# Flamingo-style stack of four gated attention and feed-forward pairs: softmax sums inverted on token partitions

## The reference, cut to what matters

```
x = x + tanh(g_xattn[l]) * attention_l(layernorm(x), ctx, ctx, ...)
x = x + tanh(g_ffn[l])   * feed_forward_l(layernorm(x), ...)

# attention, layers 0, 1 and 3: 16 heads of 8 features
scores  = einsum('bhqd,bhkd->bhqk', Q, K) ...   # with bias, causal mask or none
weights = softmax(scores, axis=-1)
out     = einsum('bhqk,bhkd->bhqd', weights, V)  # then Wo
# layer 2: 4 query heads of 32 features, one key and value head
```

## Time and profile before

| what | value |
|---|---|
| median of 3 runs | 1038.44 us (1036.83 to 1040.66) |
| profiled execution, span from first to last instruction | 1044.5 us |
| profiled execution's own device time | not recorded apart from its span |
| TensorE matmul busy | 876.9 us (84%) |
| TensorE weight load busy | 566.3 us (54%) |
| VectorE busy | 790.5 us (76%) |
| ScalarE busy | 492.8 us (47%) |
| GpSimd busy | 302.3 us (29%) |

### The profile page before, as it was taken

One profiled execution on the slowest core, in us unless ns is written; L12 is line 12 of the kernel. 1 busy time (PEld: TensorE's weight loads), 2 busy tenths in 40 slices (PEclk: granted clock), 3 DMA queues, 4 the chain that ended last, 5 costly groups with the idle time before them and its releaser, 6 DMA issues.

```text
span 1044.5 us, 19277 instructions
## 1 busy us (share of the span) xinstructions
PE 876.9 (84%) x7316; PEld 566.3 (54%) x7316; DVE 790.5 (76%) x1849; ACT 492.8 (47%) x753; POOL 302.3 (29%) x324
## 2 busy tenths in 40 slices
PE   4777867878898999987899776878888799999886
PEld 3433336534566678863565323565445575788543
DVE  6799998888774845388668998989786667455983
ACT  3655453356533422327875735433635244322575
POOL 4510245444443201110233013364534332011100
PEclk9999878898898999997999987888989898999899
DMA  9100000000000000000001000000000000000000
GB/s 318 45 3 2 2 1 1 1 3 2 2 1 1 2 1 1 1 7 7 27 27 42 1 3 1 2 1 2 3 3 1 1 2 2 1 1 1 2 8 17
DMA packets 11741, 14.26 MB, mean 14 GB/s; under 512 B 1604, under 2 KB 10716, under 8 KB 11396
## 3 DMA queue, kind: packets, MB, share of 16 engines
q1 hardware_dynamic: 11552, 12.88, 3.8%
q10 hardware_dynamic: 100, 0.14, 0.1%
HBM read 11.55 MB, written 1.05 MB: 12 GB/s over the span
## 4 chain that ended last, share of the span: by engine, by line
PE 45%; DVE 40%; ACT 7%; issue 6%; DMA 1%; POOL 1%; SPq 0%; ACTq 0%; DVEq 0%
PE banks L997 41%; DVE nm_row L1454 12%; DVE probs L1473 5%; PE banks L692 3%; DVE qf_row L1484 2%; ACT probs L953 2%; DVE st_row L1297 1%; DVE xn_row L1409 1%; DVE wide L1543 1%; DVE mv_row L1299 1%; ACT kT_row L870 1%; DVE oh_row L1519 1%; PE banks L1051 1%; DVE qr_row L1439 1%; DVE ix_row L1513 1%
## 5 line engine op out<-in xcount | busy, mean ns | idle before, releaser
L1454 DVE TENSOR_REDUCE nm_row<-banks 128x4 f32<-128x1024 f32 (+1 forms) x192 | 210.2, 1127 | 35.7 <-PE banks L997 35.1
L953 ACT ACTIVATE probs<-banks 128x1024 f32<-128x1024 f32 (+1 forms) x144 | 128.5, 932 | 40.7 <-PE banks L997 40.2
L786 POOL TENSOR_TENSOR rstd_row<-rstd_row,neghalf 128x2 f32<-128x2 f32 x66 | 47.2, 716 | 272.4 <-DVE rstd_row L1404 217.8
L997 PE MATMUL banks<-probs,vpad 128*32 128x256 f32 (+1 forms) x1536 | 110.4, 408 | 12.1 <-ACT probs L948 6.5
L997 PE MATMUL banks<-wide,c 128*128 128x256 f32 x512 | 119.9, 388 | 0.0
L997 PE MATMUL banks<-qT_row,kT_row 50*128 50x256 bf16 (+2 forms) x896 | 90.5, 298 | 28.3 <-DVE nm_row L1454 12.9
L997 PE MATMUL banks<-kT_row,qT_row 48*128 48x256 bf16 (+2 forms) x896 | 94.0, 299 | 17.4 <-DVE nm_row L1454 9.1
L997 PEld LDWEIGHTS banks<-wide,c 128*128 128x128 f32 x512 | 95.5, 192 | 15.7 <-issue 0.7
L948 ACT ACTIVATE probs<-probs 128x1024 f32<-128x1024 f32 x64 | 67.2, 1055 | 63.7 <-DVE probs L1473 62.3
L786 POOL TENSOR_TENSOR kss_row<-kss_row,neghalf 128x32 f32<-128x32 f32 x8 | 44.3, 5532 | 140.5 <-DVE kss_row L676 140.5
L997 PEld LDWEIGHTS banks<-qT_row,kT_row 50*128 50x128 bf16 (+1 forms) x896 | 41.3, 110 | 70.5 <-issue 23.5
(11 more groups left out here) (220 smaller groups left out, 1566.5 us busy)
## 6 DMA issues: line engine op xcount, KB each, us to landing
c<-in_c SPq DMA_DIRECT2D x1, 2500.0 KB
wide<-in_mask SPq DMA_DIRECT2D x8, 256.0 KB, 3.0
qT_row<-mT_row SPq DMA_DIRECT2D x96, 4.0 KB
c<-in_c SPq DMA_DIRECT2D x1, 1194.5 KB
xn_row<-in_ctx SPq DMA_DIRECT2D x8, 128.0 KB, 3.7
x_row<-in_x SPq DMA_DIRECT2D x8, 128.0 KB, 3.1
late<-in_late SPq DMA_DIRECT2D x2, 512.0 KB, 15.4
out<-x_row SPq DMA_DIRECT2D x8, 128.0 KB, 1.9
```

The costliest lines, as they stand in the source:

```text
L786: return pool.tensor_tensor(t, t, neghalf[:, 0:n], ALU.pow)
L953: act.activation(dst[:, :, 0:w], src[:, :, 0:w], ACT.Exp, scale=1.0 if l == 2 else HD ** -0.5).then_inc(sem["probs"], 1)
L997: return pe.matmul(dst, lhsT, rhs, start=start, stop=stop, **kw)
L1454: V.tensor_reduce(nm[b][:, t, :, 2 * jp:2 * jp + 2], ps[:, :, :, 0:kn], AX.X, ALU.max, negate=True).then_inc(sem["max"], 1)
```

## The change

Before, both the features and the repeated sums were made on feature partitions, and 128x256 values were inverted. Now four steps do the division:

1. `sums_flip`: TensorE multiplies `weighed_sb` (as the stationary side, 128x128) with 8 columns of `spreads`, so that the sums land with tokens on the partitions, 128x32 in a wide layer (four products, 8 columns each). In layer 2 it is two products with 4 columns of the identity, 128x8. VectorE inverts these (`rden_row`), and ScalarE widens each over its head's features into `qf_row`, 128x256.
2. `num_flip` (wide layers only): the two feature products of before; ScalarE copies the result to `oT`.
3. `o_flip`: TensorE turns the widened inverses back by two products with the identity, and VectorE multiplies them from PSUM with the features.
4. `mix` as before.

The planner's tables name the new steps with costs of their own. `LEAD` and every other entry are the same.

The step list, the costs and the PSUM banks:

```
-        out += [("divide", l, row), ("o_flip", l, row), ("mix", l, row)]
+        out += [("divide", l, row), ("sums_flip", l, row)] + ([("num_flip", l, row)] if wide else []) + [("o_flip", l, row), ("mix", l, row)]
...
-        "o_flip": [("PE", 1.03), ("DVE", 2.13)], ("o_flip", 2): [("DVE", 2.13)], "mix": [("PE", .5), ("DVE", .4)],
+        "sums_flip": [("PE", .68), ("DVE", .28), ("ACT", .27)], ("sums_flip", 2): [("PE", .34), ("DVE", .12), ("ACT", .27)],
+        "num_flip": [("PE", .46), ("ACT", .27)], "o_flip": [("PE", .35), ("DVE", .33)], "mix": [("PE", .5), ("DVE", .4)],
...
-        "o_flip": [("oT_ps", "one", "oT")] if l != 2 else [],
+        "sums_flip": [("den_ps", "one", "inverse")],
+        "num_flip": [("num_ps", "one", "num")],
+        "o_flip": [("r_ps", "one", "oT")],
```

ScalarE:

```
+                    if kind == "sums_flip":
+                        n = HEADS if l != 2 else MQ
+                        act.wait_ge(sem["inverse"], at("inverse", s))
+                        act.activation(qf[b][:, :, :].rearrange("p t (h d) -> p t h d", h=n),
+                                       rden[b][:, :, 0:n, None].to_broadcast([P, NT, n, P // n]), ACT.Copy).then_inc(sem["inverse_wide"], 1)
+                    if kind == "num_flip":
+                        evac(oT[b][:, :], "num_ps", bank("num_ps", s)[:, 0:SEQ], "num")
```

TensorE:

```
-                    if kind == "o_flip" and l != 2:
+                    if kind == "sums_flip":
 
                         pe.wait_ge(sem["sums"], at("sums", s))
-                        claim(pe, "oT_ps", s)
-                        for i, n in enumerate(("o", "r")):
-                            a, w = SPREAD_COLS[n]
+                        claim(pe, "den_ps", s)
+                        n = HEADS if l != 2 else MQ
+                        den = bank("den_ps", s)[:, 0:NT * n].rearrange("p (t h) -> p t h", t=NT)
+                        a, w = SPREAD_COLS["r"]
+                        for t in range(NT):
+                            if l == 2:
+                                ins = mm(den[:, t, :], weighed_sb[b][:, 1, t * P:(t + 1) * P], ident[:, 0:P:COLS])
+                                continue
                             for g in range(2):
-                                ins = mm(bank("oT_ps", s)[g * w:(g + 1) * w, i * SEQ:(i + 1) * SEQ], spreads[:, a:a + w],
-                                         weighed_sb[b][:, g, :])
-                        ins.then_inc(sem["oT_ps"], 1)
+                                ins = mm(den[:, t, GROUP * g:GROUP * (g + 1)], weighed_sb[b][:, g, t * P:(t + 1) * P], spreads[:, a:a + w:HD])
+                        ins.then_inc(sem["den_ps"], 1)
+                    if kind == "num_flip":
+                        claim(pe, "num_ps", s)
+                        a, w = SPREAD_COLS["o"]
+                        for g in range(2):
+                            ins = mm(bank("num_ps", s)[g * w:(g + 1) * w, 0:SEQ], spreads[:, a:a + w], weighed_sb[b][:, g, :])
+                        ins.then_inc(sem["num_ps"], 1)
+                    if kind == "o_flip":
+                        pe.wait_ge(sem["inverse_wide"], at("inverse_wide", ("sums_flip", l, row)))
+                        claim(pe, "r_ps", s)
+                        for t in range(NT):
+                            ins = mm(bank("r_ps", s)[:, t * P:(t + 1) * P], qf[b][:, t, :], ident)
+                        ins.then_inc(sem["r_ps"], 1)
```

VectorE:

```
+                    if kind == "sums_flip":
+                        dve.wait_ge(sem["den_ps"], at("den_ps", s))
+                        n = HEADS if l != 2 else MQ
+                        V.reciprocal(rden[b][:, :, 0:n], bank("den_ps", s)[:, 0:NT * n].rearrange("p (t h) -> p t h", t=NT)).then_inc(sem["inverse"], 1)
                     if kind == "o_flip":
-                        over = qf[b][:, :, :].rearrange("p t d -> p (t d)")
-                        if l == 2:
-                            dve.wait_ge(sem["sums"], at("sums", s))
-                            num, den = weighed_sb[b][:, 0, :], weighed_sb[b][:, 1, :]
-                        else:
-                            dve.wait_ge(sem["oT_ps"], at("oT_ps", s))
-                            ps = bank("oT_ps", s)
-                            num, den = ps[:, 0:SEQ], ps[:, SEQ:2 * SEQ]
-                        ch.link(V.reciprocal(over, den))
-                        V.tensor_tensor(oT[b][:, :], num, over, ALU.mult).then_inc(sem["oT"], 1)
+                        dve.wait_ge(sem["r_ps"], at("r_ps", s))
+                        if l != 2:
+                            dve.wait_ge(sem["num"], at("num", ("num_flip", l, row)))
+                        num = weighed_sb[b][:, 0, :] if l == 2 else oT[b][:, :]
+                        V.tensor_tensor(oT[b][:, :], bank("r_ps", s)[:, 0:SEQ], num, ALU.mult).then_inc(sem["oT"], 1)
```

More of the change, by code:

```diff
@@ L199, in starts_after @@
         out.append((("consts", 0, ROWS - 1), "SP"))
-    if l >= 1 or kind in ("attend", "o_flip", "route", "choose", "spread", "fore", "outer"):
+    if l >= 1 or kind in ("attend", "sums_flip", "num_flip", "o_flip", "route", "choose", "spread", "fore", "outer"):
         if eng != "SP":
@@ L215, in starts_after @@
                 "weigh": [(of("attend", l, 2 * (part or 0) + n), "POOL" if l == 1 else "ACT") for n in range(2)],
-                "o_flip": [(of("divide", l), "ACT")], "mix": [(of("o_flip", l), "DVE")],
+                "sums_flip": [(of("divide", l), "ACT")], "num_flip": [(of("divide", l), "ACT")], "o_flip": [(of("sums_flip", l), "ACT")], "mix": [(of("o_flip", l), "DVE")],
                 "route": [(of("flip", 4 + l), "ACT")],
@@ L230, in starts_after @@
                 "norm": [(of("stats", l), "POOL")],
-                "o_flip": [(of("divide", l), "ACT")] if l == 2 else [],
+                "o_flip": [(of("num_flip", l), "ACT")] if l != 2 else [],
                 "mix": [(of("plus", l), "POOL")],
@@ L319, in signals @@
                 "q_turn": ["q_ready"], "q_mid": ["q_rest"], "q_low": ["q_stack"],
-                "max": ["max"], "shift": ["shift"], "attend": ["biased"], "o_flip": ["oT"], "mix": ["x_mixed"],
+                "max": ["max"], "shift": ["shift"], "attend": ["biased"], "sums_flip": ["inverse"], "o_flip": ["oT"], "mix": ["x_mixed"],
                 "route": ["logits", "gate_in"] if l == 1 else ["logits", "onehot"], "gate": ["onehot"],
@@ L328, in signals @@
                 "shift_flip": ["shiftT"], "attend": ["probs"] + (["v_placed"] if wide and s[3:] == (0,) else []),
-                "divide": ["sums"], "route": ["gate_exp"], "choose": ["onehotT"] + (["u"] if l == 1 else []),
+                "divide": ["sums"], "sums_flip": ["inverse_wide"], "num_flip": ["num"], "route": ["gate_exp"], "choose": ["onehotT"] + (["u"] if l == 1 else []),
                 "inner": ["h0"], "again": ["h1"], "deep": ["ht"]}[kind]
@@ L550, in build @@
         rms = each("rms", [P, NT])
+        rden = each("rden", [P, NT, HEADS])
         qss = each("qss", [P, NT * HEADS])
```

## The result

The changed kernel takes 1056.6 us, the median of 4 runs (1053.23 to 1062.62); the kernel before took 1037.63 us on the same chip (4 runs, 1034.75 to 1040.66). The ratio is 1.0188, with a 95% interval of 1.0142 to 1.0233: slower by 1.9%. The profiled execution has a span of 1057.2 us where the one before had 1044.5.

The account below looks back on a forecast made before the run. Neither TensorE nor VectorE was taken to bound the whole kernel. VectorE-led -10.3, TensorE-led +9.3, mixed -2.1 and path +6.3 us gave +3.2 on 1038.44: 1041.6 us, called no change; range 1022.5 to 1059.

Parts of the forecast that it names:

- Durations: New steps' prices: reciprocals on a line through two measured sizes; VectorE saves 46 us, TensorE gains 37, ScalarE 22.
- VectorE-led term: Layer 0 stretches, VectorE 92% busy: 8 wide divisions with shorter reciprocals save 10.3 us, TensorE's added work covered by idle time.
- TensorE-led term: Layer 2 and the experts around it, TensorE 98% busy: 8 narrow divisions' added products cost 9.3 us.
- the faster rival: TensorE takes its new work in its gaps, so both TensorE terms vanish: 1022.5 us; chance 0.26.
- The path: Mixed stretches: each row's division enters three more in-order queues; 7 divisions on the chain at 0.9 us, +6.3 us.
- The slower rival: Rows' products wait 2.0 us longer behind other rows' work on VectorE in 8 divisions, +16 us: 1054 us; chance 0.28.
- the first theory: Written for the experiments: the four rewritten lists make the loss; the new arithmetic alone is worth about nothing or a gain.

Follow-up runs that it names:

- the first experiment: The changed kernel's lists with the old division (two spreading products, 128x256 reciprocal), no thin products, widening or turn back: 1068.61 us, 1.0305 of the kernel before.
- the fitted ninth: The changed kernel, wide and narrow divisions changed, with turn back by transposes, corrected planner costs and leads fitted by search: 1029.22 us, 0.9896 of the kernel before.
- The control: The kernel before, arithmetic untouched, with other leads found by the same search: 1041.64 us, 1.004 of the kernel before.
- the third run: The kernel before, arithmetic untouched, with each lead moved by about 2 us: 1064.8 us, 1.0267 of the kernel before.
- the sixth run: The changed kernel with the planner's costs corrected towards measured ones and then the leads fitted: 1048.13 us, 1.0111 of the kernel before.
- the fourth run: The changed kernel with each lead moved by about 2 us: 1090.0 us, 1.0494 of the kernel before.
- the seventh's: The changed kernel in its own lists, with the turn back issued as two transposes instead of products with the identity: two runs, 1049.65 and 1062.84 us.

## Why the prediction was wrong where it was

The range, 1022.5 to 1059.0, held the time; the forecast, no change, did not come. Step by step:

*Durations: right.* Reciprocals 351 and 202 ns where the line gave 353 and 203. VectorE's busy time fell by 44.7 us (46 said), TensorE's rose by 33.4 (up to 37 said). Thin products 1.06 us (1.02), features 0.65 (0.54), turn back 0.71 (0.68), widening 0.412 (0.4). ScalarE gained 17.9 us (22).

*VectorE-led term, -10.3 us: not shown, and too large in the lists of the change.* It depends on the window. From the first to the fifth division the time went from 142.9 to 138.3 us and from the seventeenth to the twentieth from 66.6 to 60.9, together -10.3; but these two do not match. Up to the next layer in both sets of rows, first to fifth and seventeenth to twenty-first, it is -4.6 and +6.0 (139.9 to 145.9), and without that passage, first to fourth and seventeenth to twentieth, +6.1 (63.8 to 69.9) and -5.7. The clean comparison is the first experiment with the changed kernel, the same lists with the old and the new arithmetic: 140.7 and 146.0 us against 138.3 and 145.9, a gain of 2.5 us. In the fitted ninth the matching windows are 137.5 and 137.4, 7.9 us less than before.

*TensorE-led term, +9.3 us: too large.* From the ninth to the thirteenth division it was 150.6 us before and 149.0 after; from the twenty-fifth to the twenty-ninth 148.1 and 153.9, together +4.2. In the same lists with the old arithmetic (the first experiment) they are 147.3 and 155.8, so there the new arithmetic costs nothing in them (-0.3). With the narrow work undone in the same lists nothing to 2 us came back, and fitted, the kernel with narrow divisions changed is about 4 us faster than the two without (1029.2 against 1033.6 and 1033.1, of which the clock explains some: 1030.4 against 1029.5 and 1032.8 at 0.906). So the narrow part is worth about nothing either way; it isn't a cost of 9 us. The busy share of 98% did not mean that added products add their length, which is what the faster rival had said. The undoing gives VectorE its long reciprocals back, so what these pairs measure is the narrow part as a whole. By the rule of the Trainium skill that stood there (Perfetto Trace Analysis, Identifying the Most-Contended Engine: weight load time tells the headroom) the term would be small, and that agrees with these runs, though none of them isolates the reason.

*The path, +6.3 us: mechanism seen, cost not.* At the end of the program the path from the first product to the start of `mix` is now 1049.90 to 1053.18, 3.28 us (3.22 said). In the queues it is longer: summed over the 32 divisions, from the start of the reciprocal to the end of the product, 145.3 us after and 70.6 before, 4.5 us each where 2.2 was; at the first it is 6.35 where 4.2 was said. But in the ninth experiment, the fastest of all, it is 161.4 us, the longest. The detour doesn't decide the time, at least not in fitted lists.

*The slower rival: its price near (1054), its mark absent.* It was to decide where the residual step's wait grew by more than 10 us; it fell from 25.3 to 20.4. By that mark, and by the ninth experiment, its mechanism isn't what made the loss. VectorE did wait more in front of the division, 53.0 us where it was 25.4, in lists that had changed too. That the time came out beside its number is no support.

*The step that failed* is one that the sum does not have: "other steps moved in the lists too, with the leads unchanged" stood there only as an argument for a rival, and the sum priced it at nothing. The runs show that it is the largest term. The change with lists fitted to it is 9 us below the kernel before, 1029.2 against 1038.1, and the change as made 19 us above (1056.6 against 1037.6): 28 us for the order and the transposition together. What the transposition has of it in fitted lists was not measured; its saved TensorE time is 7.7 us. The lists of the change with the old arithmetic cost 31 us. The control found no such gain for the kernel before (+0.4%), with one other set of leads, and the third run shows that it would lose as much by leads off by 2 us. In the lists of the change the arithmetic alone is a gain of 4.2 us at one clock (12.0 as timed); the three terms of the sum without the path were -10.3 + 9.3 - 2.1 = -3.1 us. That they come near is luck, since the first two are both too large.

*Open.* Which steps stall in the lists of the change between the twentieth and the twenty-first division and behind it isn't settled. Nor is all of what separates the sixth run (1048.1) from the ninth (1029.2): they differ in transposes, in the cost of the turn in the play, and in leads, so in all their lists. Of the 19 us the play shows 5.7 (1003.2 and 997.4). Fitted leads for the whole change gave 1029, 1048 and 1051 us on the chip, so part of the ninth's margin may be luck among orders. And with the leads moved by 2 us in both kernels the change still cost 25 us, which the first theory does not explain; the play there is 8.1 us longer for the change (1032.4 against 1024.3).

## What to carry to other kernels

Where a planner writes the order, an edit of the arithmetic is two changes, and the second is the larger: correct the planner's costs to measured ones and fit the order again before judging the edit, and hold the lists fixed to see the arithmetic alone. Look at the length of the planner's own play before and after the edit, with measured costs: here it showed 11 us of loss with the costs that the edit came with, and 22 with the corrected ones. Find first how far the time moves when only the order does (one run with leads off by 2 us gave 27 us here); a forecast without that term has no business with a range narrower than it. A rival is confirmed by its mark in the trace, never by its number coming near; and a window that is to test a term is chosen by the same rule in every place, or it finds the number that it looks for.

## What was unexpected of the hardware

- The same TensorE work has no fixed busy time. The changed kernel's 7572 products are busy 910.3 us in one order and 931.0 in another (the fourth run); the ninth run's 7508 take 902.2 and the seventh's 7508 take 911.2. The granted clock may be part of it, 0.874 in the fourth run's profile and 0.906 in the changed kernel's, but it isn't all: the ninth's and the seventh's clocks are 0.900 and 0.898, and in the third run, the kernel before with moved leads, TensorE is busy 876.5 us at 0.895 where it was 876.9 at 0.909.
- The order goes with another clock, not only other idle time: from 0.908 to 0.889 (before, other leads, one chip) and from 0.906 to 0.874 (the change, other leads), means over the runs. By the slope of 5.6 us for 0.01 some 10 of the 27 us and 19 of the 33 go with it, by the 1.7 of the kernel before 3 and 5. Which comes first, idle time or the lower clock, was not tried.
- A reciprocal costs 6.24 ns an element of the free dimension from 8 to 256 elements: 202, 351 and 1751 ns lie on one line. The long one takes the same from PSUM and from SBUF; the short ones read PSUM here.
